# The first feed-forward layer written as one block, with its deviations made in the attention before it

## What is computed

```python
def quantize_a16(x):
    amax = jnp.clip(jnp.max(jnp.abs(x)), 1e-08, None)
    scale = 32767.0 / amax
    return jnp.clip(jnp.round(x * scale), -32768.0, 32767.0) / scale   # straight-through form left out
x = x + jnp.tanh(g_xattn[0]) * _L0_xattn_ref(_layernorm(x), ctx_1024, ...)
# _L0_ffn_ref, on n = _layernorm(x):
hidden = jax.nn.gelu(quantize_a16(n) @ W_in_sim + b_in, approximate=False)   # 128 -> 512
out = quantize_a16(hidden) @ W_out_sim + b_out                               # 512 -> 128
x = x + jnp.tanh(g_ffn[0]) * out
```

## Time and profile before

| what | value |
| --- | --- |
| median of 3 runs | 1602.4 us (1601.57 to 1603.79) |
| the profiled execution, its own time | 1600.68 us |
| its span | 1599.1 us |
| PE busy over the span | 1447.5 us, 91% |
| DVE, ACT, POOL busy | 1088.4 (68%), 902.2 (56%), 623.2 us (39%) |
| the 40 slices, PE | `6999999999999996559789999899989999987996` |
| mean granted clock of PE | 0.968 |

### The profile page before, as it was taken

How to read it: one execution, slowest core, us unless ns; L and a number is a source line. 1 busy time by engine, 2 the same in 40 slices (tenths; PEclk the granted TensorE clock), 3 DMA queues, 4 the chain that set the end, 5 groups by cost and what they waited for, 6 DMA issues and landing times. The chain is left out here.

```text
span 1599.1 us, 27379 instructions
## 1 busy us (share of the span) xinstructions
PE 1447.5 (91%) x9078; PEld 1200.0 (75%) x9094; DVE 1088.4 (68%) x2356; ACT 902.2 (56%) x1903; POOL 623.2 (39%) x747
## 2 busy tenths in 40 slices
PE   6999999999999996559789999899989999987996
PEld 4888888888888875229767878787878787766884
DVE  5676776776777776898655757575656566774886
ACT  3666666666666653660155656565656565545662
POOL 1233434334334333840113333333433342445885
PEclk9999999999999998899899999999999999998998
DMA  8544444444444422000064444444444444320111
GB/s 260 176 157 133 140 153 131 160 130 153 133 154 130 151 77 78 25 0 0 18 202 134 133 131 131 133 131 136 133 129 133 135 124 135 106 68 1 33 33 40
DMA packets 198329, 182.27 MB, mean 114 GB/s; under 512 B 14144, under 2 KB 195392, under 8 KB 198208
## 3 DMA queue, kind: packets, MB, share of 16 engines
q1 hardware_dynamic: 197632, 180.60, 35.9%
q10 hardware_dynamic: 576, 0.13, 0.0%
HBM read 95.43 MB, written 84.93 MB: 113 GB/s over the span
## 5 line engine op out<-in xcount | busy, mean ns | idle before, releaser
L911 POOL TENSOR_TENSOR PN<-E,RC 128x512 f32<-128x512 f32 (+1 forms) x384 | 336.3, 904 | 581.7 <-DVE RC L869 581.7
L823 DVE TENSOR_REDUCE MX<-pS 128x6 f32<-128x462 f32 (+1 forms) x384 | 221.9, 578 | 256.2 <-PE pS L573 256.0
L608 PE MATMUL pO<-work,PT 128*128 128x128 f32 (+1 forms) x2560 | 333.9, 278 | 15.9 <-ACT PT L711 15.9
L662 ACT ACTIVATE G<-pP 128x308 f32<-128x308 f32 (+1 forms) x488 | 209.0, 429 | 244.8 <-PE pP L514 244.4
L608 PEld LDWEIGHTS pO<-work,PT 128*128 128x128 f32 (+1 forms) x2560 | 312.4, 194 | 23.0 <-issue 20.5
L573 PE MATMUL pS<-G,XT 128*128 128x462 f32 (+1 forms) x768 | 324.4, 507 | 0.0
L702 ACT ACTIVATE E<-E 128x462 f32<-128x462 f32 (+1 forms) x384 | 209.6, 546 | 151.0 <-DVE E L833 142.3
L512 PE MATMUL pP<-Chi,Ahi 128*128 128x308 f32 x496 | 240.4, 485 | 1.4 <-ACT G L662 1.2
L593 PE MATMUL pT<-ident,PN 128*128 128x128 f32 (+1 forms) x1280 | 203.8, 278 | 32.7 <-POOL PN L911 31.7
L833 DVE TENSOR_TENSOR E<-pS,MX 128x462 f32<-128x462 f32 (+1 forms) x384 | 223.6, 582 | 9.1 <-issue 0.2
L711 ACT ACTIVATE PT<-pT 128x512 f32<-128x512 f32 (+1 forms) x384 | 200.5, 523 | 47.4 <-PE pT L593 47.3
(11 more groups left out here) (194 smaller groups left out, 1948.7 us busy)
## 6 DMA issues: line engine op xcount, KB each, us to landing
values<-ST SPq DMA_DIRECT2D x256, 256.0 KB
work<-values SPq DMA_DIRECT2D x512, 128.0 KB
values<-ST SPq DMA_DIRECT2D x64, 208.0 KB
work<-values SPq DMA_DIRECT2D x128, 104.0 KB
C<-in_ctx SPq DMA_DIRECT2D x32, 154.0 KB
out<-s_O SPq DMA_DIRECT2D x16, 256.0 KB, 2.3
work<-in_L_xattn_Wq SPq DMA_DIRECT2D x2, 512.0 KB, 7.5
work<-in_L_xattn_Wkv SPq DMA_DIRECT2D x2, 512.0 KB, 8.0
```

The source lines that it names most:

```text
L608: last = nc.tensor.matmul(pO[:, 0:CH], PT[0:rows, c, :], V[(t - 1) % VRING][0:rows, tile, CH * hh:CH * hh + CH], start=c == 0, stop=c == C ...
L662: return nc.scalar.activation(G[0:live, g % 2, :, head, :], bank[0:live, 0:KEYCOLS].rearrange("p (b k) -> p b k", k=KEYS), ACT.Copy)
L823: nc.vector.tensor_reduce(MX[:, h0:h1], pS[u][:, 0:(h1 - h0) * KEYS].rearrange("p (h k) -> p h k", k=KEYS), X_AXIS, ALU.max).then_inc(max_ ...
L911: nc.gpsimd.tensor_tensor(out, e, scale, ALU.mult).then_inc(prob_ready, 1)
```

## The change

In attention 0, DVE writes mean and variance straight into `p["mv"]`, adds epsilon per group, and POOL raises to -0.5 per group, as layer 1 does; the order of the reductions changes. The first feed-forward becomes one block in place of three, without loops. Its scale needs no square root. A maximum crosses the partitions in one matmul: the column is read as a broadcast 128 x 128 left operand against the identity, so that every row of the result holds all 128 values. Rounded inputs keep their offset until after the turn; ACT's copy and DVE's difference take it off there, so a group is rounded in one pass. ACT loads the Gelu table ahead with a dummy call. POOL adds the bias rows after it has normalised all 16 groups. The turns of the raw weights move behind group 1, their copies behind the last Gelu and their difference before the last residual. XN, XQ, HI, LO and the raw weights share memory with the hidden quantiser's buffers.

```diff
@@ attention, statistics_after (both layers) @@
+                dve.wait_ge(bn2_done, g + 1)
+                for b in range(GROUP):
+                    last = nc.vector.bn_aggr(p["mv"][:, g * GROUP + b, :], BN[:, b, :])
+                last.then_inc(mv2_done, 1)
                 if layer == 0:
                     nc.vector.tensor_reduce(p["rowmax"][:, rows], p["X"][:, rows, :], X_AXIS, ALU.max)
+                dve.wait_ge(mv2_done, g + 1)
+                nc.vector.tensor_scalar(p["rs"][:, rows], p["mv"][:, rows, 1], EPS, None, ALU.add).then_inc(ve2_done, 1)
+                if layer == 0:
                     nc.vector.tensor_reduce(p["rowmin"][:, rows], p["X"][:, rows, :], X_AXIS, ALU.min)
-                nc.vector.tensor_copy(p["mv"][:, rows, :], MV2[:, :, :])
...
-                if layer == 1 and b == 2 and group >= 1:
+                if b == 2 and group >= 1:
                     deviation_after(group - 1)
-            if layer == 1:
-                deviation_after(GROUPS - 1)
+            deviation_after(GROUPS - 1)
@@ quantised_ffn, POOL @@
+            def normalise(g):
+                half, rows = g % 2, slice(g * GROUP, (g + 1) * GROUP)
+                if g >= 2:
+                    pool.wait_ge(xq_ready, g - 1)
...
+            for g in range(GROUPS):
+                normalise(g)
+            pool.wait_ge(gbias_made, 1)
+            for g in range(GROUPS):
+                rows = p["X"][:, g * GROUP:(g + 1) * GROUP, :]
+                nc.gpsimd.tensor_tensor(rows, rows, gbias[:, :].unsqueeze(1).to_broadcast([128, GROUP, CH]),
+                                        ALU.add).then_inc(biased, 1)
@@ PE @@
+            def across(n):
+                nc.tensor.matmul(pX[0][:, 0:128], peak[:, n:n + 1].to_broadcast([128, 128]), p["ident"][:, :],
+                                 start=True, stop=True).then_inc(spread, 1)
...
+            pe.wait_ge(step_, RANGE)
+            across(0)
+            turn(0)
+            for g in range(GROUPS):
+                if g + 1 < GROUPS:
+                    turn(g + 1)
+                pe.wait_ge(hi_out, g + 1)
+                pe.wait_ge(lo_out, g + 1)
                 for c in range(FC):
+                    wait(pe, gelu_done, g * FC + c - FC + 1)
...
+                if g == 1:
+                    pe.wait_ge(raw_in, 32)
+                    for c in range(FC):
+                        n = slice(128 * c, 128 * c + 128)
+                        nc.tensor.transpose(pF[:, n], raw_fc[:, c, :], p["ident"][:, :])
+                        last = nc.tensor.transpose(pP[:, n], raw_proj[:, n], p["ident"][:, :])
+                    last.then_inc(raw_turned, 1)
+            pe.wait_ge(step_, RANGE + SCALE + 1)
+            across(1)
@@ ACT @@
+                nc.scalar.activation(HI[g % 2], pX[g % 2][:, :], ACT.Copy, bias=-ROUND).then_inc(hi_out, 1)
+            act.wait_ge(gate_in, 16)
+            nc.scalar.activation(gate[:, :], gcol[:, :], ACT.Tanh).then_inc(tanh, 1)
+            nc.scalar.activation(warm[:, :], gcol[:, :], ACT.Gelu)
@@ DVE @@
+            def scale_from(s):
+                done(nc.vector.tensor_reduce(s[:, 1:2], pX[0][:, 0:128], X_AXIS, ALU.max))
+                done(nc.vector.tensor_scalar(s[:, 1:2], s[:, 1:2], 1e-8, 1.0 / 32767.0, ALU.max, ALU.mult))
+                done(nc.vector.reciprocal(s[:, 0:1], s[:, 1:2]))
+            def quantise(g):
+                dve.wait_ge(xn_ready, g + 1)
+                wait(dve, xq_turned, g - 1)
+                nc.vector.tensor_scalar(XQ[g % 2], XN[g % 2], sx[:, 0:1], ROUND, ALU.mult, ALU.add).then_inc(xq_ready, 1)
+            def low(g):
...
+                nc.vector.scalar_tensor_tensor(out=LO[g % 2], in0=pX[g % 2][:, :], scalar=ROUND, in1=HI[g % 2],
+                                               op0=ALU.subtract, op1=ALU.subtract).then_inc(lo_out, 1)
...
+            nc.vector.tensor_tensor(up[:, :], p["rowmax"][:, :], p["mv"][:, :, 0], ALU.subtract)
+            done(nc.vector.tensor_tensor(down[:, :], p["mv"][:, :, 0], p["rowmin"][:, :], ALU.subtract))
+            done(nc.vector.tensor_tensor(up[:, :], up[:, :], down[:, :], ALU.max))
+            done(nc.vector.tensor_tensor(up[:, :], up[:, :], p["rs"][:, :], ALU.mult))
+            done(nc.vector.tensor_reduce(peak[:, 0:1], up[:, :], X_AXIS, ALU.max))
+            dve.wait_ge(spread, 1)
+            scale_from(sx)
+            quantise(0)
+            nc.vector.tensor_scalar(in_scale[:, :], inv[:, 0, :], sx[:, 1:2], None, ALU.mult).then_inc(scaled, 1)
+            quantise(1)
+            low(0)
...
+            def residual(g):
+                dve.wait_ge(down_ready, g + 1)
+                dve.wait_ge(biased, g + 1)
...
+            quantise_hidden(1)
+            done(nc.vector.tensor_scalar(small[:, :], sh[:, 1:2], gate[:, 0:1], None, ALU.mult))
+            for g in range(2, GROUPS):
+                residual(g - 2)
+                quantise_hidden(g)
+            residual(GROUPS - 2)
+            dve.wait_ge(fhi_out, 1)
+            nc.vector.tensor_tensor(spiking["Flo"][:, :], pF[:, :], spiking["Fhi"][:, :].bitcast(F32), ALU.subtract)
+            residual(GROUPS - 1)
```

More of the change, by code:

```diff
@@ L966, in quantised_ffn @@
[L966 to L977, removed]
@@ new lines, in half_of @@
+        def half_of(i, first, n):
+            return HALVES[:, i, 512 * first:512 * (first + n)]
+        XN = [half_of(0, i, 1).rearrange("p (b d) -> p b d", d=CH) for i in range(2)]
+        XQ = [half_of(0, 2 + i, 1).rearrange("p (b d) -> p b d", d=CH) for i in range(2)]
+        HI = [half_of(1, i, 1).bitcast(BF16)[:, 0:512] for i in range(2)]
+        LO = [half_of(1, i, 1).bitcast(BF16)[:, 512:1024] for i in range(2)]
+        raw_fc = half_of(1, 2, 1).rearrange("p (c d) -> p c d", d=CH)
@@ new lines, in quantised_ffn @@
+        centred, xn_ready, xq_ready, xq_turned, hi_out, lo_out, up_ready, gelu_done = (
+            sem(n) for n in ("centred", "xn_ready", "xq_ready", "xq_turned", "hi_out", "lo_out", "up_ready", "gelu_done"))
+        step_, spread, tanh, scaled, gbias_made, biased = (
+            sem(n) for n in ("step", "spread", "tanh", "scaled", "gbias_made", "biased"))
+        added, hq_ready, down_ready, x_done = (sem(n) for n in ("added", "hq_ready", "down_ready", "x_done"))
+        block = s.enter_context(nc.Block())
@@ new lines, in _ @@
+        @block.sync
+        def _(sp):
+            sp.dma_start(gcol[:, :], w["gate"].partition_broadcast(128)).then_inc(gate_in, 16)
+            sp.dma_start(brow[:, :], w["b_out"].partition_broadcast(128)).then_inc(bias_in, 16)
+            with nc.allow_non_contiguous_dma("512 bias values, once"):
+                sp.dma_start(b_in[:, :], w["b_in"].rearrange("(c p) -> p c", p=128)).then_inc(up_bias_in, 16)
+            sp.dma_start(raw_fc, spiking["W_fc"].rearrange("(c p) d -> p c d", p=128)).then_inc(raw_in, 16)
+            sp.dma_start(raw_proj, spiking["W_proj"]).then_inc(raw_in, 16)
+            load_weights(sp, p, next_w, next_loaded)
@@ new lines, in _, with high @@
+        @block.scalar
+        def _(act):
+            def high(g):
+                act.wait_ge(xq_turned, g + 1)
+                if g >= 2:
+                    act.wait_ge(up_ready, (g - 1) * FC)
+                nc.scalar.activation(HI[g % 2], pX[g % 2][:, :], ACT.Copy, bias=-ROUND).then_inc(hi_out, 1)
+            act.wait_ge(gate_in, 16)
+            nc.scalar.activation(gate[:, :], gcol[:, :], ACT.Tanh).then_inc(tanh, 1)
+            nc.scalar.activation(warm[:, :], gcol[:, :], ACT.Gelu)
+            high(0)
+            act.wait_ge(up_bias_in, 16)
+            act.wait_ge(scaled, 1)
+            for g in range(GROUPS):
+                if g + 1 < GROUPS:
+                    high(g + 1)
+                for c in range(FC):
+                    act.wait_ge(up_ready, g * FC + c + 1)
+                    nc.scalar.activation(HID[:, g, c, :], pU[c][:, :], ACT.Gelu, bias=b_in[:, c:c + 1],
+                                         scale=in_scale[:, c:c + 1]).then_inc(gelu_done, 1)
+            act.wait_ge(raw_turned, 1)
+            nc.scalar.activation(spiking["Fhi"][:, :], pF[:, :], ACT.Copy).then_inc(fhi_out, 1)
+            nc.scalar.activation(spiking["WP"][:, :, :].rearrange("p c d -> p (c d)"), pP[:, :], ACT.Copy)
```

396 lines of the change are left out of this document (99 added, 297 removed).

## The result

The changed kernel takes 1586.0 us, the median of four runs (1584.6 to 1586.4), beside 1602.0 for the kernel before (1599.6 to 1603.8, four runs). The ratio is 0.990, with a 95% interval of 0.988 to 0.992: 16.0 us less, between 13 and 19. The forecast was 1582.2, 20.2 less. The profiled execution took 1586.39 us and its span is 1584.5. One slow execution of the kernel before, 3225 us, in the set that b_mask, a_mask, a_nobias and a_inter were measured with, is left out of all medians and ratios.

What follows compares the result with a forecast made beforehand. PE was taken to bound attention 0 and the down block, DVE the up block's steady part. First hidden rounding -22.2, additions +3.5, loops -1.5 gave -20.2: 1602.4 - 20.2 = 1582.2 us, range 1576.5 to 1589.

Steps and rivals of the forecast that it cites:

- rival 2: Up loop: it keeps meeting POOL and a group stays at 3.65 us; 1586.4 us in all, chance 0.17.
- Attention 0 at no cost: Attention 0: the 16 powers added on POOL cost 0, except the last, which ends the block 0.45 us later.
- rival 3: Attention 0: the added powers delay it by 15.3 us; 1597.5 us in all, chance 0.04.
- Block start to first Gelu: Feed-forward start: with one crossing and no square root, the first Gelu comes at 638.9, 12.1 us earlier.
- the contention of the small steps: Feed-forward start: POOL's subtraction delays DVE's small two-input steps by 1.0 us, between 0 and 2.1.
- The up loop: Up block: a group takes 3.25 us instead of 4.08, all Gelus 51.1 instead of 60.24, 9.1 less.
- Hidden maximum and chain: Behind the last Gelu: maximum at 693.0, 21.1 us earlier; then 1.9 instead of 3.07 to the first hidden rounding.
- The collision of the additions: Down block start: POOL's last bias additions delay the first four hidden rounding passes, +3.5 us, between 0 and 5.
- rival 4: Down block: PE's clock stays low, 3.57 us more per group; 1639 us with all sixteen groups, chance 0.05.
- Rival 1: Down block start: POOL's bias additions cost nothing; 1578.7 us in all, chance 0.20.
- Loops: Down block: without loops seven loop turns of 0.23 us go, taken as -1.5 us, between 0 and -1.7.
- in layer 1: 0: Layer 1: only a copy goes there, so the change costs or gains 0.

Runs made afterwards that it cites:

- b_mask: The kernel before, with each mask of attention 1 loaded one group earlier on SP's queue: 1557.9 us, ratio 0.972.
- a_mask: The changed kernel, with each mask of attention 1 loaded one group earlier on SP's queue: 1538.6 us, ratio 0.960 to the kernel before.
- a_nobias: The changed kernel, with only the first of POOL's sixteen bias additions in the first feed-forward: 1582.7 us, ratio 0.988 to the kernel before.
- a_inter: The changed kernel, with POOL's bias additions back beside the up loop, one behind each normalisation: 1590.7 us, ratio 0.992 to the kernel before.
- a_poolwait: The changed kernel, with POOL's first normalisation held until DVE's third small step: 1581.0 us, one run.
- b_onepass: The kernel before, with only the single rounding pass of the change: 1599.8 us, ratio 0.999.
- a_warm: The changed kernel, with 24 idle matmuls for PE in the fold of layer 1: 1579.5 us, ratio 0.985 to the kernel before.
- b_warm: The kernel before, with 24 idle matmuls for PE in the fold of layer 1: 1601.3 us, ratio 0.999.
- am_hold: a_mask, with POOL's normalisation held until DVE's third small step and its last four bias additions held into the down block: 1536.1 us, ratio 0.958.
- the best version: am_hold with the idle matmuls for PE in the fold of layer 1: 1535.6 us, ratio 0.958 to the kernel before.

## Why the prediction was right, and where it was not

The direction and the place of the gain were right, and so was its size inside the feed-forward. The changed kernel is at 1586.0, inside the range. It is 3.8 above the forecast, and the forecast's -20.2 lies outside the measured interval of -13 to -19. The number is that of rival 2 (1586.4), but that is chance: its mechanism, a group of 3.65, did not occur.

**Attention 0 at no cost: right.** Its first residual starts 0.89 earlier than before and its last 0.86 earlier, so the 15 powers between them cost nothing that shows, and rival 3 is out. The block begins 0.50 later behind the last residual; 0.45 was taken.

**Block start to first Gelu: 11.1 earlier, not 12.1.** The step that failed is the contention of the small steps. I took 1.0, between 0 and 2.1, and it was 2.4, above both ends. The bound was too low because I counted two POOL instructions and the steps met three. The Trainium skill, SBUF — State Buffer, section "SBUF: two separate sides", has a DVE instruction with two SBUF inputs and a GpSimd instruction exclude each other for their whole length. The estimate by it, 1.6, was nearer, the trace agrees with the rule (0.22 alone in a_poolwait, 0.95 to 1.10 beside POOL), and I weighed it too lightly. A part came back: the second rounding met no POOL instruction (635.34, 0.48 long). The single crossing took 0.96 where 0.85 was taken, and the table load lies off the path at 632.62. The terms named from the second rounding to the first Gelu add up to 638.6 at most and not to 638.9: ACT's copy between the turn and the products, 0.60 in rows 4, is not named.

**The up loop: right.** A group of 3.19 against 3.25, and 51.13 for all Gelus against 51.1. b_onepass shows that "DVE bounds it" was a wrong reading of the kernel before, though. The sum came out because it was built from the group's links and had POOL's additions gone, and because the 0.91 was known to be POOL's doing. The single pass in the old loop is worth 0.05 a group; in the new block, with the additions still beside it, the group is at 3.42, and with them moved at 3.19. So, as far as these runs go, the pass pays only where the ring isn't closed. In every profile with the move the steady group is at 3.19. The changed kernel with the old two passes was not run, so what the pass is worth there isn't measured.

**Hidden maximum and chain: right.** The chain took 1.89 against 1.9. The maximum ends 20.2 earlier in place of 21.1, the miss of the first Gelu carried on.

**The collision of the additions: right in kind, too dear, and not alone.** Three passes met POOL, not four. The first residual lost 2.7 behind the first hidden rounding where 3.5 was taken, but by a_nobias only 1.9 of that is the additions'. The other 0.9 (7.24 against 6.38) goes with PE's lower clock there, 0.60 against 0.69: a little of rival 4, in the first hidden group. Rival 1, that the additions cost nothing, is out by a_nobias: 2.5 in the whole feed-forward.

**Loops: 0.9, not 1.5.** The spacing of residuals is 3.63 and 3.57 in turn, where the loop had 3.79 and 3.56. The last one still has 2.23 of idleness before it, so the raw weights' difference fits, as said.

These errors partly cancel, and that is luck. Inside the feed-forward the sum was -20.2 and the trace has -19.6. Of the chances, 0.94, 0.01 and 0.05 don't fit the list of rivals, which leaves 0.95 for faster by more and 0.05 for all of rival 4.

**The step that failed: "in layer 1: 0", and with it the silent step that what follows the block is only shifted.** It cost 3.7 in the fold and 2.5 in attention 1. The first is the mechanism of rival 4, PE's clock, at a place where I had not looked: in the down block the clock is 1.00 from the first residual to the last. The second is a wait for a transfer whose length depends on the moment at which it is met. a_mask against b_mask (-19.3 in medians, -20.3 in spans) shows that the change is worth about what the sum says once the masks are out of the way, though the spans without the start of attention 0 differ by 17.9 only, since the fold still takes 2.2. a_warm against b_warm, with the fold's clock lifted in both, gives -21.8 and -23.1, and of the latter 2.6 are again the masks (42.5 against 45.1), which leaves 20.5; the feed-forward there is 21.1 shorter.

How long the fold takes goes with PE's mean clock in it in all fourteen profiles: 67.3 to 67.5 at a mean of 0.82, 66.0 at 0.84, 65.0 at 0.87, 63.8 and 63.9 at 0.89, 63.7 and 63.9 at 0.92, and 62.8 to 63.2 at 0.95 and 0.97. What stays open is why the same fold gets a lower clock behind the changed feed-forward. It isn't chance: 67.4 and 67.5 in two profiles of it, 63.7 and 63.9 in two of before. But small edits elsewhere in the feed-forward move it too: 62.8 in a_nobias, 65.0 in a_poolwait and am_hold, 66.0 in a_mask. No run here tells what sets it.

## What to carry to other kernels

Before saying that an engine bounds a loop because it is always busy, take out of its instructions the time for which another engine holds them up (the same shape, alone, elsewhere in the trace); what is left may be a ring, in which a pass less gives nothing until the other engine has less to do or another phase. When a chain in front of a big queue is shortened, allow for what the code behind it does at the new moment: here two stretches of almost unchanged code gave back 6 of 20 us, through PE's clock and through one late transfer. And read the waits view of the whole kernel for short waits that recur: fourteen waits for 308 bytes were worth more than twice the whole change, and three lines took them away.

## What the runs showed of the hardware

- DVE's instructions with two SBUF inputs and its rounding passes are held up by a POOL tensor operation that they meet: 64 columns in 0.95 to 1.10 instead of 0.22, a rounding of 512 columns in up to 1.50 instead of 0.48, one of 2048 columns in 1.73 instead of 1.28. All of it counts as DVE's busy time. The reductions are not: a maximum of 2048 columns took 2.27 to 2.29 each time, beside POOL's work (656.62 above) and, in a_nobias, without it.
- PE's granted clock in a stretch doesn't follow from the code of that stretch alone: 0.51 and 0.83 in the same 10 us of the fold, and 1.00 with 24 idle matmuls about it or, in a_nobias, with 15 additions of POOL gone in the feed-forward. In am_hold it was 0.50 for 6 us in which PE was busy 5.75, at the start of the down block:
```profile
697.00:703.00 6.00, 5.75 (x27) 5.75 (x28) 5.20 (x10) 0.00 (x0) 0.00 (x0) 0.50 0.00 0
```
- Idle matmuls that lift the clock to 1.00 where it was low are worth something only there: in the fold 4.5 us in the changed kernel, 0.5 to 0.7 in the one before and 2.1 in the best version. In the medians that is 6.5 (some of it the masks'), nothing measurable, and 0.5.
